# The last stage of a two-layer network: gate broadcasts and biases on groups of 32 rows, and GpSimd's work placed by the steps of a choice

## The reference

```python
def _L1_ffn_ref(x, router_w, router_b, expert_w, expert_b):   # D = C = 64, E = 8, K = 2
    router_probs = jax.nn.softmax(x @ router_w + router_b, axis=-1)
    top_p, top_i = jax.lax.top_k(router_probs, K)
    top_p = top_p / jnp.sum(top_p, axis=-1, keepdims=True)
    expert_out = jnp.einsum('bnd,edc->bnec', x, expert_w) + expert_b
    gathered = jnp.take_along_axis(expert_out, top_i[..., None], axis=2)
    return jnp.einsum('bnk,bnkc->bnc', top_p, gathered)
...
x = x + _L1_conv_ref(_ln_c(x), ...)
t = _to_tokens(x)
t = t + _L1_ffn_ref(_ln_t(t), L1_ffn_router_w, L1_ffn_router_b, L1_ffn_expert_w, L1_ffn_expert_b)
```

## Time and profile before

| | us |
|---|---|
| median of 3 runs | 2174.63 (2174.14 to 2175.13) |
| the profiled execution | 2173.03 |
| its span, first to last instruction | 2171.2 |

### The profile page before, as it was taken

The page is one execution under the profiler, slowest core; times in us unless marked ns, Lnnn a source line. Parts: engine busy times, 40 slices in busy tenths (PEclk is TensorE's granted clock), DMA queues, the critical chain, the costliest instruction groups (busy, mean ns, idle before and its releaser), DMA issues. The chain is left out here.

```text
span 2171.2 us, 40393 instructions
## 1 busy us (share of the span) xinstructions
PE 2062.0 (95%) x14350; PEld 1585.6 (73%) x14350; DVE 1239.5 (57%) x2610; ACT 971.3 (45%) x2751; POOL 511.1 (24%) x591
## 2 busy tenths in 40 slices
PE   6999991799999989999999999999998999999999
PEld 3555550377777789999999999999997555555554
DVE  5777778566666643222222222222223999999998
ACT  4666664334444423333444444444445343334331
POOL 4555543322222200000000000000002545444441
PEclk9999995599999999999999999999998999999999
DMA  4955541222222200000000000000002455555553
GB/s 118 241 161 166 169 144 32 74 98 93 89 93 98 89 12 1 0 0 0 1 2 0 0 0 0 20 0 0 0 0 73 122 138 141 136 140 138 136 125 78
DMA packets 192800, 159.05 MB, mean 73 GB/s; under 512 B 25977, under 2 KB 159129, under 8 KB 192665
## 3 DMA queue, kind: packets, MB, share of 16 engines
q1 hardware_dynamic: 190968, 156.91, 26.0%
q0 software_dynamic: 512, 0.53, 0.1%
q10 hardware_dynamic: 1184, 0.00, 0.0%
HBM read 56.72 MB, written 67.11 MB: 57 GB/s over the span
## 5 line engine op out<-in xcount | busy, mean ns | idle before, releaser
L1207 PE MATMUL s_ps<-g_ring,g_T 128*128 128x128 f32 x7620 | 856.8, 275 | 7.9 <-DVE g_ring L1254 7.9
L1207 PEld LDWEIGHTS s_ps<-g_ring,g_T 128*128 128x128 f32 x7620 | 855.7, 192 | 8.7 <-DVE g_ring L1254 8.5
L1243 DVE SCALAR_TENSOR_TENSOR g_ring<-s_ps,s_xs 128x128 f32<-128x128 f32 x508 | 148.3, 292 | 422.3 <-PE s_ps L1207 422.3
L1671 DVE TENSOR_TENSOR tm_Z<-tm_pg,tm_nd 128x1024 f32<-128x1024 f32 x256 | 298.8, 1208 | 12.4 <-PE tm_pg L1525 12.4
L1306 ACT ACTIVATE g_X<-g_ring 128x256 f32<-128x256 f32 x254 | 172.2, 678 | 298.7 <-DVE g_ring L1243 298.7
L1537 PE MATMUL tm_po<-tm_Z,g_wexp 128*64 128x512 f32 x1024 | 247.7, 605 | 0.0
L1290 ACT ACTIVATE g_X<-g_ring 64x256 f32 x256 | 106.9, 417 | 203.4 <-DVE g_ring L1243 201.2
L1243 DVE SCALAR_TENSOR_TENSOR g_ring<-s_ps,g_X 128x128 f32<-128x128 f32 x254 | 74.0, 292 | 209.4 <-PE s_ps L1207 209.4
L1301 ACT ACTIVATE s_xs<-g_X 128x256 f32<-128x256 f32 x254 | 161.3, 636 | 0.6 <-PEq L1183 0.6
L1618 POOL TENSOR_TENSOR g_X<-g_x,g_X 128x512 f32<-128x512 f32 x64 | 84.8, 1344 | 287.2 <-POOLq L1183 287.2
L1525 PE MATMUL tm_pg<-tm_gT,g_sel 96*128 96x512 f32 x512 | 147.5, 409 | 1.1 <-DVE tm_Z L1671 1.0
(11 more groups left out here) (276 smaller groups left out, 2946.9 us busy)
## 6 DMA issues: line engine op xcount, KB each, us to landing
tm_nd<-g_X SPq DMA_DIRECT2D x256, 128.0 KB, 2.4
g_X<-in_x SPq DMA_DIRECT2D x128, 128.0 KB, 2.9
x1s<-g_X SPq DMA_DIRECT2D x64, 256.0 KB, 2.1
x1tok<-g_X SPq DMA_DIRECT2D x64, 256.0 KB, 2.4
g_x<-x2s SPq DMA_DIRECT2D x64, 256.0 KB, 2.9
y<-tm_yo SPq DMA_DIRECT2D x128, 128.0 KB, 2.5
g_X<-x1s SPq DMA_DIRECT2D x32, 256.0 KB, 2.7
x2s<-g_X SPq DMA_DIRECT2D x32, 256.0 KB, 2.0
```

The lines of the kernel that those rows point to most:

```text
L1207: last = pe.matmul(out, g.T[i][:, d * P:d * P + P], g.ring[(u - 1) % RING][:, images(c), d:d + 64], start=(d == 0), stop=(d == ND - 1))
L1243: dve.scalar_tensor_tensor(g.ring[n % RING][:, images(c), inner], conv, 0.0, x[:, images(c)], ALU.max, ALU.add).then_inc(y_ready[c], 1)
L1671: dve.tensor_tensor(Z[q % 4][:], pg[q % 2][:].rearrange("p (h n) -> p h n", h=2), nd[t % 2][i][:], ALU.mult).then_inc(s["z"], 1)
```

## The change

The two matmuls of a broadcast use one group of 32 rows each: `sel` and `gT` have the scaled gates on rows 0 to 31 and, for the other half, once more on rows 64 to 95, which ACT copies with a second instruction. The plain gates stand on rows 32 to 63 (`PLAIN`). The bias becomes two matmuls on these (the rounded bias and its rest), each with 32 rows, one ahead of each broadcast of parts 0 and 2. The turned gates have 64 columns in place of 96, and `split` loses its last instruction.

```diff
+                        at, rows = h * E1 + 2 * ep, slice(h * C, h * C + 2 * G2)
+                        last = pe.matmul(pg[q % 2][:, h * N:h * N + N], sel[rows, at:at + 2].rearrange("p e c -> p (e c)"),
+                                         gT[i][rows], start=True, stop=True)
...
-                def biases(t, i):
-                    wait(pe, s["y"], 2 * t + i - 1)
-                    pe.matmul(po[i][:], bias[:], gT[i][:], start=True, stop=False, skip_group_check=True)
+                def biases(t, i, part):
+                    if part == 0:
+                        wait(pe, s["y"], 2 * t + i - 1)
+                    pe.matmul(po[i][:], bias[PLAIN, part], gT[i][PLAIN], start=(part == 0), stop=False,
+                              skip_group_check=True)
...
-                        if now(ex) and p % 2 == 0:
-                            biases(ex, p // 2)
                         for q in (2 * p + 2, 2 * p + 3):
+                            if now(ex) and p % 2 == 0:
+                                biases(ex, p // 2, q % 2)
...
-                    act.activation(gT[i][:], bankB[0:ROWS, :], ACT.Copy).then_inc(s["gcopied"], 1)
+                    act.activation(gT[i][0:C], bankB[0:C, :], ACT.Copy)
+                    act.activation(gT[i][C:C + 2 * G2], bankB[0:2 * G2, :], ACT.Copy).then_inc(s["gcopied"], 1)
```

The two subtractions of a maximum from L move to POOL (`lower`, semaphores `shifted` and `lowered`); the comparison with the second maximum and its product with `rev` become one instruction, as for the first. `choose` has 11 instructions, numbered anew, and they stand behind other products. POOL's list is put in another order, and a part of it waits for a numbered instruction of the choice:

```diff
+                def lower(t, links, done):
+
+                    pool.wait_ge(chain, t * LINKS + links)
+                    pool.tensor_tensor(L[:], L[:], over(m1[:]), ALU.subtract).then_inc(s[done], 1)
...
                 for t in range(STEPS):
+                    if now(t - 2):
+                        weigh(t - 2)
                     if now(t - 1):
                         scale(t - 1)
                     if now(t - 2):
                         split(t - 2)
+                    if now(t - 1):
+                        lower(t - 1, 1, "shifted")
+                        pool.wait_ge(chain, (t - 1) * LINKS + 5)
                     if now(t + 1):
                         x3(t + 1, 0)
+                    if now(t - 1):
+                        lower(t - 1, 6, "lowered")
+                    if now(t + 1):
                         x3(t + 1, 1)
-                    if now(t - 1):
-                        weigh(t - 1)
 
             @block.vector
             def _(dve):
...
+                    elif n == 4:
+                        dve.wait_ge(s["exp"], t + 1)
                         before(4)
                         linked(dve.scalar_tensor_tensor(L[:], F1[:], NEVER, L[:], ALU.mult, ALU.add), 5)
...
-                slots = [(), (0, 1, 2, 3, 4), (5, 6), (7, 8, 9, 10)]
-
                 for t in range(STEPS):
-                    for p in range(EP):
+                    for q in range(UNITS):
                         if now(t - 3):
-                            z_of(t - 3, 2 * p)
-                            z_of(t - 3, 2 * p + 1)
-                        if now(t - 4) and p == 0:
+                            z_of(t - 3, q)
+                        if now(t - 2) and q == 0:
+                            choose(t - 2, 9)
+                            choose(t - 2, 10)
+                        if now(t - 4) and q == 1:
                             y_of(t - 4, 1)
-                        if now(t - 2) and p == 0:
-                            choose(t - 2, 11)
-                            choose(t - 2, 12)
                         if now(t - 1):
-                            for n in slots[p]:
+                            for n in {1: (0,), 3: (1, 2, 3, 4), 5: (5,), 7: (6, 7, 8)}.get(q, ()):
                                 choose(t - 1, n)
-                        if now(t - 3) and p == 2:
+                        if now(t - 3) and q == 5:
                             y_of(t - 3, 0)
```

More of the change, by code:

```diff
@@ L151, in load_mixture @@
         load(g.rt[h * C:h * C + C, h * E1:h * E1 + E1], a["router_w"])
-    for q in range(12):
+    for q in range(4, 8):
         load(g.bn[q * E1:q * E1 + E1], a["expert_b"])
@@ L1331, in blank_mixture @@
         pool.memset(g.rev[:, e:e + 1], float(E1 - e))
[L1332 to L1333 removed]
+    pool.memset(g.sel[:].bitcast(F32), 0.0).then_inc(g.mix_blank, 1)
 def fold_centre(pe, g, out):
@@ L1360, in prepare_mixture @@
         dve.wait_ge(g.mix_chain, BLOCKS)
-        dve.tensor_copy(g.sel[0:2 * G2], bcast(g.r16[0:2 * G2], 2, C))
+        for rows in (slice(0, 2 * G2), slice(C, C + 2 * G2)):
+            dve.tensor_copy(g.sel[rows], bcast(g.r16[rows], 2, C))
     elif n == BLOCKS + 2:
@@ L1415, in top2_mixture @@
         GG = m.sb("GG", [P, 2, 2 * TILES, G2])
-        gp = [m.sb(f"gp{u}", [P, 2 * TILES, 3, 2, G2], F32R) for u in range(2)]
-        gT = [m.sb(f"gT{i}", [ROWS, N], F32R) for i in range(2)]
+        gp = [m.sb(f"gp{u}", [P, 2 * TILES, 2, 2, G2], F32R) for u in range(2)]
+        gT = [m.sb(f"gT{i}", [P, N], F32R) for i in range(2)]
         bankA, bankB = m.ps("bankA"), m.ps("bankB")
@@ L1645, in split @@
                     link(pool.tensor_tensor(scaled, plain, over(R[u][:]), ALU.mult))
-                    link(pool.tensor_tensor(gp[u][:, :, 0:2, 0], both, none, ALU.add))
-                    link(pool.tensor_tensor(gp[u][:, :, 0:2, 1], both, gp[u][:, :, 0:2, 0].bitcast(F32), ALU.subtract))
-                    pool.tensor_tensor(gp[u][:, :, 2], gp[u][:, :, 1].bitcast(F32), none, ALU.add).then_inc(s["gates"], 1)
+                    link(pool.tensor_tensor(gp[u][:, :, :, 0], both, none, ALU.add))
+                    pool.tensor_tensor(gp[u][:, :, :, 1], both, gp[u][:, :, :, 0].bitcast(F32), ALU.subtract
+                                       ).then_inc(s["gates"], 1)
                 x3(0, 0)
@@ L1714, in choose @@
                         linked(dve.tensor_reduce(m1[:], L[:], AXX, ALU.max), 6)
+                    elif n == 6:
+                        dve.wait_ge(s["lowered"], t + 1)
+                        linked(dve.scalar_tensor_tensor(A_[:], L[:], 0.0, revb, ALU.is_equal, ALU.mult), 7)
                     elif n == 7:
-                        before(6)
-                        linked(dve.tensor_tensor(A_[:], L[:], over(m1[:]), ALU.is_equal), 7)
+                        before(7)
+                        linked(dve.tensor_reduce(m1[:], A_[:], AXX, ALU.max), 8)
@@ L1718, in choose @@
                     elif n == 8:
-                        before(7)
-                        linked(dve.tensor_tensor(A_[:], A_[:], revb, ALU.mult), 8)
+                        before(8)
+                        dve.tensor_tensor(F2[:], A_[:], over(m1[:]), ALU.is_equal).then_inc(s["chosen"], 1)
                     elif n == 9:
-                        before(8)
-                        linked(dve.tensor_reduce(m1[:], A_[:], AXX, ALU.max), 9)
+                        dve.wait_ge(s["weighed"], t + 1)
@@ L1724, in choose @@
+                        linked(dve.tensor_reduce(total[:], F1[:], AXX, ALU.add), 9)
                     elif n == 10:
                         before(9)
-                        dve.tensor_tensor(F2[:], A_[:], over(m1[:]), ALU.is_equal).then_inc(s["chosen"], 1)
-                    elif n == 11:
-                        wait(dve, s["weighed"], t + 1)
-                        linked(dve.tensor_reduce(total[:], F1[:], AXX, ALU.add), 10)
-                    elif n == 12:
-                        before(10)
```

42 lines of the change are left out of this document (17 added, 25 removed).

## The result

The changed kernel takes **2231.03 us** (median of 4 runs, 2226.84 to 2233.85), against 2174.87 (2174.14 to 2175.13) for the kernel before in the same comparison: a ratio of **1.026, 95% interval 1.0247 to 1.0273**. It is slower, as forecast, but by 56 us and not by 19, and it lies above the range. The profiled execution took 2233.85 us; its span is 2232.0.

A forecast was written before the change was run, and what follows sets the result against it. PE was taken to bound the mixture at 15.29 us a step, DVE 0.3 us behind. Loop +22.3, end -4.5, start +1 gave +18.8 on the 2174.6 median: 2193 us, range 2180 to 2213.

The forecast's parts named there:

- The moved wait closes a loop: Mixture: lowering's wait for EX, now ahead of z4, closes a DVE-PE-ACT circle of 16.06 us against 15.29; +22.3 us over 29 steps.
- DVE's idle time ahead of L1722: Sign in the mixture: about 2 us of waiting before the lowering, ended by ACT's EX, 29 times.
- The terms of the loop: Mixture step, six stretches between products, tiles and EX: 2.80 + 3.47 + 2.55 + 2.80 + 1.63 + 2.81 = 16.06 us.
- The Trainium skill's rule on the switches: PE's changes of tiling mode: by the rule both new switches drain the engine, step 0.1 to 0.3 us longer, 2196 to 2202.
- 32-row groups run side by side: PE's broadcasts: the two matmuls of a unit overlap, 0.235 us a unit instead of 0.47.
- The rival without overlap: PE's broadcast pairs run singly: loop 16.77 us, +43 us, 2217; chance 0.14, shared with any other cost above 2205.
- The clock falls: PE waits some 2.6 us of 16, so its clock may drop; several us a step, no chance of its own.
- PE's busy share: Sign in the mixture: PE busy about 85%, its broadcasts waiting for Z.
- The collision of POOL and DVE: Two DVE instructions, means 891 and 586 ns, become short if POOL is idle beside them; same-size one takes 0.29 us.
- Ends and start: Mixture's last halves save -4.5 us; its start costs about +1 (0 to 2.5) because `x3` waits for the choice.

The follow-up runs named there:

- late_lowering: Changed kernel with the instruction lowering the first maximum put back behind z5 on DVE, and POOL's wait moved along; 2146.05 us, ratio 0.989 to the kernel before.
- exp_first: Changed kernel with ACT making EX before it reads the new tiles; 2146.52 us, ratio 0.9893 to the kernel before.
- choice_only: Changed kernel's choice and POOL order, with the 96-row broadcasts and the bias of the kernel before; 2216.08 us, ratio 1.0207 to the kernel before.
- late_sum: late_lowering with the sum of the weights and its reciprocal behind z1 in place of z0; 2132.57 us, ratio 0.9815 to the kernel before.
- rows_pinned: rows_only with one more wait on POOL ahead of `x3`; 2140.32 us, ratio 0.9857 to the kernel before.
- rows_only: Changed kernel's 32-row matmuls and shorter `split`, with the choice and POOL order of the kernel before; 2224.45 us, ratio 1.0249 to the kernel before.
- late_free_x3: late_lowering without POOL's wait ahead of the first `x3`; 2157.70 us, ratio 0.9931 to the kernel before.

## Why the prediction was right in direction and wrong in size

- **The moved wait closes a loop: right, and shown.** DVE's idle time ahead of L1722 is 2.44 us in the step above, ended by EX, for "about 2 us" forecast; the list of groups gives 51.4 us over 21. It goes when the loop is opened at either end (late_lowering, exp_first), and stays without the 32-row groups (choice_only).
- **The terms of the loop: two kinds too small.** 16.43 for 16.06. Three of the terms hold PE's change of work: twice +0.1 from a product's end to the tiles and +0.09 from tiles to z0, about 0.3 together; ACT's reads of the tiles are the other 0.09 (the two terms with DVE's products err by +0.01 and -0.03). In the start of the mixture, from which I took them, PE went from the broadcasts to 96-column turned gates in 0.58 and on in 0.53; here broadcasts to turned gates take 0.44 (0.58 less 0.235 would be 0.35), and turned gates to experts 0.56. I had put nothing for that switch. All of the 0.37 makes +10 us over 28 steps, and with it the forecast would have stood at 2203, inside the range.
- **The Trainium skill's rule on the switches:** "TensorEngine Tiling (Array Packing)", Key Properties, says that a change of the tile mode, and not just of the tile, drains the engine. By it I had 0.1 to 0.3 us more a step. The trace agrees in kind: about 0.3 more.
- **32-row groups run side by side: right.** The two records of a pair start 3 to 4 ns apart in the trace, and four broadcasts take 0.66 us in late_sum's chain, where 96-row ones took 0.93. The rival without overlap is out.
- **"The clock falls ... I keep it in the upper tail": here the prediction failed.** The condition was named rightly (PE waits, rows show nothing between 100% busy and idle), but it got no price and no chance of its own. What came were 14 stretches at half clock that cost 1.6 to 3.3 us each, +27.5 us, and 4.7 more in the first step: as much as the whole loop. From rows of before a price could have been estimated. Turned gates and experts take 0.44 + 1.87 = 2.31 us on the loop; if they double at half clock, that is up to 2.3 us a step, 32 us over 28 steps if it hits half of them and 64 if it hits all. With +32 the upper tail begins at 2225, and the range would have had to go there. How many steps it hits, no row of before could say.
- **What the waits and the kinds of matmul do together** was not in the forecast at all. In these runs it takes both: waits with 96-row matmuls (choice_only) and 32-row ones almost without waits (late_lowering, rows_pinned, late_sum) keep full clock; both together (the change, rows_only) lose it; and 128-row filling, not 32-row filling, brings it back. Not run are 96-row matmuls with waits as long as the change has, and fills that differ in rows alone. So that the clock's loss comes from waits and kind of work together is shown, and that the rows are what counts in the kind is argued.
- **PE's busy share: 85% forecast, 42.59 / 47 = 91% measured.** The trace shows waits of 0.83 and 0.63 ahead of broadcasts, 1.46 a step and not 2.6: records of the bias, whose ends lie in the waits, count as busy.
- **The collision of POOL and DVE: right that it goes** (L1718 has a mean of 292 ns in the changed kernel, L1711 too), **wrong on what it is worth.** I took 0.3 and 0.6 us for it from the earlier trace rows, hidden. One such collision can cost 1.0 us of DVE's time, and rows_only shows two of them setting the step. That the shorter `split` alone moves `x3` 0.72 us forward, onto them, I hadn't seen; in the change POOL's new wait kept this from happening.
- **Ends and start: right in sign.** The last two steps and the end gave -3.4 for -4.5 forecast. The mixture begins 1.6 us earlier. Its first step is 6.4 us slower where about +1 was forecast, for `x3`; `x3` isn't on its chain of waits, the loop is, and 4.7 us of half clock.

## What to carry to other kernels

When an instruction is moved ahead of the work that used to cover its wait, follow that wait back through every list in order until it ends at data that doesn't depend on the mover: if it comes back to the same engine, add up the circle, and compare the sum with the busiest engine's step. When waits open up on TensorE, give the clock a price and a chance of its own, above all where its matmuls use few rows of the array. And an instruction taken out of one engine's list moves all that stands behind it: here it put GpSimd's two-input work onto VectorE's, and one wait that pins it was worth 84 us.

## What the runs showed of the hardware

- **The granted clock depends on the kind of matmuls, as well as on waits; the rows in use are the nearest reading.** Over 360 us with 14.8 and 15.3 us of PE idle time, it was 0.96 with 32-row filling and 1.00 with 128-row filling; 1.00 with 19.1 us idle and 96-row broadcasts; 0.94 and 0.92 with 33.5 and 34.0 us idle and 32-row ones. No single wait of PE was over 0.85 us in the undisturbed stretch shown, 1841 to 1888 us, at the end of which the clock fell from the 2.4 to the 1.2 GHz level, and none over 1.12 us in the 360. Experts that take 1.87 us at full clock took 3.04 in the stretch at half.
- **A short VectorE instruction with two inputs in SBUF ended only behind GpSimd's two-input addition beside it.** In late_free_x3 it ended 0.15 us behind it; in rows_only L1708 ended at 1881.05 and the additions at 1880.91, 0.14 behind. The price is thus not a factor, but what is left of GpSimd's instruction: 0.29 us become 1.27 (mean of 21) or 1.37 (mean of 24). Not held were the products, which read PSUM (mean 1.21 us in rows_only as in the changed kernel), nor, in the trace of before, the reduction L1703, 0.29 us at 1918.73, beside additions from 1918.52 to 1921.19.
- **Side-by-side groups of 32 rows:** starts 3 to 4 ns apart, four broadcasts of 512 columns in 0.66 us, about 0.1 us for a switch to another group size or back.
